# The expert choice of a fused attention and mixture-of-experts kernel, cut into two parts, with its small products at the end of their slot

## What is computed

```python
x = x + xattn(layernorm(x), ctx)      # 64 batches of 128 rows, 256 wide; 16 heads of 64; ctx is 192 wide
x = x + moe(layernorm(x))             # all 8192 rows

def moe(tokens):
    probs = softmax(tokens @ gate_w.T)                   # 8 experts
    top2_w, top2_idx = top_k(probs, 2)
    expert_out = silu(tokens @ expert_w[e].T + expert_b[e])
    mixed = sum of the two chosen expert_out, weighted by top2_w
    return mixed @ combine_w.T
```

## Time and profile before

| | us |
|---|---|
| median of three runs | 1540.31 |
| lowest, highest | 1539.81, 1540.96 |
| the profiled execution, its time | 1538.33 |
| the profiled execution, its span | 1536.6 |
| PE busy | 1489.9 (97%) |
| DVE busy | 1291.6 (84%) |
| ACT busy | 1061.8 (69%) |
| POOL busy | 939.1 (61%) |

### The profile page before, as it was taken

One profiled execution on the slowest core, in us unless ns is written; L12 is line 12 of the kernel. 1 busy time (PEld: TensorE's weight loads), 2 busy tenths in 40 slices (PEclk: granted clock), 3 DMA queues, 4 the chain that ended last, 5 costly groups with the idle time before them and its releaser, 6 DMA issues.

```text
span 1536.6 us, 38493 instructions
## 1 busy us (share of the span) xinstructions
PE 1489.9 (97%) x11680; PEld 1433.8 (93%) x11680; DVE 1291.6 (84%) x3129; ACT 1061.8 (69%) x2929; POOL 939.1 (61%) x1237
## 2 busy tenths in 40 slices
PE   6989999999999999999999999999999999999898
PEld 6989999999899999999999999989999999999887
DVE  7888888888988888888988888888888888987677
ACT  5766776766677667676677667766767667677665
POOL 4666666666655555587766455657666656655644
PEclk8999999999999999999999999999999999999999
DMA  6643443333577777544578777647887778887853
GB/s 183 201 152 94 108 110 97 94 94 97 162 226 209 220 217 223 159 114 140 172 230 244 217 231 232 203 117 220 243 250 237 230 228 248 251 243 216 285 183 110
DMA packets 181596, 287.78 MB, mean 187 GB/s; under 512 B 23697, under 2 KB 116881, under 8 KB 181137
## 3 DMA queue, kind: packets, MB, share of 16 engines
q1 hardware_dynamic: 170640, 255.94, 57.0%
q0 software_dynamic: 10752, 29.37, 6.1%
HBM read 156.51 MB, written 61.60 MB: 142 GB/s over the span
## 4 chain that ended last, share of the span: by engine, by line
PE 77%; DVE 14%; issue 3%; ACT 2%; SPq 2%; DMA 1%; POOL 0%; DVEq 0%; ACTq 0%; POOLq 0%
PE gen_ps L595 20%; PE qk_ps L595 17%; PE o_ps L595 10%; PE s_ps L595 10%; PE proj_ps L595 9%; PE pT_ps L636 6%; DVE sums L1073 2%; PE gen_ps L714 2%; PE gen_ps L681 2%; DVE neg_max L1066 2%; DVE pT_s_lo L1008 1%; DVE qk_s L1008 1%; PE gen_ps L689 1%; DMA k_s<-qk_s 1%; DVE xn L1053 1%
## 5 line engine op out<-in xcount | busy, mean ns | idle before, releaser
L851 ACT ACTIVATE stage<-s_ps,neg_max 128x128 f32<-128x128 f32 x1024 | 293.7, 376 | 32.1 <-DVE neg_max L1066 31.1
L1405 POOL CAST o_s_hi<-stage 128x256 fp32r<-128x256 f32 x256 | 102.5, 400 | 342.8 <-ACT stage L825 340.9
L1396 POOL TENSOR_TENSOR stage<-stage,inv_sums 128x512 f32<-128x512 f32 x256 | 266.1, 1039 | 36.8 <-DVE inv_sums L1075 36.4
L825 ACT CAST qk_s<-qk_ps 128x512 fp32r<-128x512 f32 x256 | 150.8, 589 | 134.3 <-PE qk_ps L595 132.7
L1066 DVE TENSOR_REDUCE neg_max<-s_ps 128x4 f32<-128x512 f32 x256 | 176.4, 689 | 66.6 <-PE s_ps L595 62.4
L595 PE MATMUL s_ps<-k_s,qk_s 128*128 128x256 f32 x1536 | 226.7, 284 | 2.8 <-DMA k_s<-qk_s 2.2
L1008 DVE TENSOR_TENSOR pT_s_lo<-pT_ps,pT_s_hi 128x512 fp32r<-128x512 f32 x256 | 173.7, 678 | 45.7 <-ACT pT_s_hi L825 41.4
L595 PEld LDWEIGHTS s_ps<-k_s,qk_s 128*128 128x128 f32 x1536 | 201.8, 189 | 3.5 <-DMA k_s<-qk_s 2.8
L1407 POOL TENSOR_TENSOR o_s_lo<-stage,o_s_hi 128x256 fp32r<-128x256 f32 x256 | 189.4, 740 | 20.8
L825 ACT CAST v_s_hi<-gen_ps 128x512 fp32r<-128x512 f32 x129 | 75.8, 588 | 179.4 <-PE gen_ps L595 179.4
L825 ACT CAST pT_s_hi<-pT_ps 128x512 fp32r<-128x512 f32 x256 | 150.4, 588 | 64.4 <-PE pT_ps L636 60.3
(11 more groups left out here) (385 smaller groups left out, 4695.2 us busy)
## 6 DMA issues: line engine op xcount, KB each, us to landing
w_block<-expert_table SPq DMA_DIRECT2D x147, 512.0 KB
k_s<-qk_s SPq DMA_DIRECT2D x512, 128.0 KB
stage<-sorted_x SPq DMA_DIRECT2D x147, 128.0 KB
sorted_y<-stage SPq DMA_DIRECT2D x147, 128.0 KB, 4.0
x_raw<-in_x SPq DMA_DIRECT2D x32, 256.0 KB
c_raw<-in_ctxT SPq DMA_DIRECT2D x32, 256.0 KB, 3.9
stage<-in_x SPq DMA_DIRECT2D x32, 256.0 KB, 3.7
x_kept<-x SPq DMA_DIRECT2D x32, 256.0 KB
```

Of the source, the lines that this page charges most:

```text
L825: last = act.copy(to, of)
L851: last = act.activation(probs[p % 2][:, k, :], s_ps[:, k * P:(k + 1) * P], ACT.Exp, bias=neg_max[p % 2][:, k:k + 1])
L1396: pool.tensor_tensor(probs[b][:, :, :], probs[b][:, :, :], inv_sums[b][:, :].unsqueeze(2).broadcast_to([P, 4, P]), ALU.mult).then_inc(prob ...
L1405: pool.tensor_copy(hi[:, :, :], o_full).then_inc(o_hi, 1)
```

## The change

The choice is cut in two, and three things move.

- On VectorE `route_top` ends with the copy to floats, which now raises a semaphore of its own (`top_copied`) instead of making VectorE wait. What stood behind it, `picks` and the two instructions for `hot`, is now `route_hot`, and stands in slot 7 between `row_max` and `qk`.
- On TensorE the `rank` products are the last general job of slot 7, behind `attend`, `project`, and the late jobs. The order of general jobs sets the banks, so the banks of the jobs in slot 7 and what each job waits for change too.
- On VectorE `route_rows` and `rows_end` stand in slot 0 of the next pair, behind the mid jobs. GpSimd writes nothing out in slot 0 and two of the four parts in slot 1.

```diff
--- before.py
+++ after.py
@@ -109,10 +109,10 @@
         self.jobs_at, order = {}, []
         for s in range(-SLOTS, self.last + 1):
             i, u = s // SLOTS, s % SLOTS
-            early, mid, late = [], [], []
+            early, mid, late, last = [], [], [], []
             for kind, k, off in ATTENTION_JOBS.get(u, []):
                 if 0 <= i + off < (SPARSE if kind == "rank" else pairs):
-                    mid.append((kind, (i + off) * per(kind) + k))
+                    (last if kind == "rank" else mid).append((kind, (i + off) * per(kind) + k))
             if s in self.turn:
                 early.append(("turn_block", self.turn[s][2]))
             if s - 1 in self.mix:
@@ -121,6 +121,7 @@
                 late.append(("expert", self.turn[s - 1][2]))
             if s - 2 in self.mix:
                 late.append(("combine", self.mix[s - 2]))
+            late += last
             self.jobs_at[s, "early"], self.jobs_at[s, "mid"], self.jobs_at[s, "late"] = early, mid, late
             order += early + mid + late
         self.place = {job: n for n, job in enumerate(order)}
@@ -313,8 +314,8 @@
         proj_ps = stack.enter_context(nc.psum_tensor("proj_ps", [P, 512], F32))
         gen_ps = [stack.enter_context(nc.psum_tensor(f"gen_ps{b}", [P, 512], F32)) for b in range(BANKS)]
 
-        x_in, c_in, xres_in, gate_in, bias_in, biased = (
-            sem(n) for n in ("x_in", "c_in", "xres_in", "gate_in", "bias_in", "biased"))
+        x_in, c_in, xres_in, gate_in, bias_in, biased, top_copied = (
+            sem(n) for n in ("x_in", "c_in", "xres_in", "gate_in", "bias_in", "biased", "top_copied"))
         w_in = [sem(f"w_in{n}") for n in range(18)]
         table_stored = [sem(f"table_stored{r}") for r in range(RING)]
         last_in = [sem(f"last_in{r}") for r in range(RING)]
@@ -1129,9 +1130,12 @@
                 for t in range(2):
                     last = dve.max_index(top_at[:, t, :], top8[:, t, :], logits[:, t, :])
                 link(last)
-                link(dve.tensor_copy(top_atf[:, :, :], top_at[:, :, 0:2]))
+                dve.tensor_copy(top_atf[:, :, :], top_at[:, :, 0:2]).then_inc(top_copied, 1)
+
+            def route_hot(j):
                 if j == 0:
                     dve.wait_ge(w_lo_pool, PROJ_BY_POOL)
+                dve.wait_ge(top_copied, j + 1)
                 picks = chosen_of(j)
                 link(dve.tensor_tensor(picks, expert_no[:, 0:E].unsqueeze(1).broadcast_to([P, 4, E]),
                                        top_atf[:, :, :].rearrange("p t k -> p (t k)").unsqueeze(2).broadcast_to([P, 4, E]),
@@ -1265,10 +1269,6 @@
                         split_lo(hi_of[kind], n + 1, [(lo, bank[:, 0:N2], hi)], drained[kind])
                     elif kind == "gate":
                         gate_logits(n, bank)
-                    elif kind == "rank":
-                        route_rows(n, bank)
-                        if n + 1 in plan.ends:
-                            rows_end(plan.ends.index(n + 1), n)
 
             for e in range(REGIONS):
                 dve.memset(expert_no[:, e:e + 1], float(e))
@@ -1307,6 +1307,8 @@
                     row_max(i, u + 1)
                 if u == 7 and nxt:
                     row_max(i + 1, 0)
+                if u == 7 and before:
+                    route_hot(i - 1)
                 if u < 5 and now:
                     qk(i, u + AHEAD)
                 if u >= 5 and nxt:
@@ -1316,6 +1318,10 @@
                     for n in range(FOR_FIRST):
                         weight_lo(n)
                 general(s, "mid")
+                if u == 0 and 0 <= i - 2 < SPARSE:
+                    route_rows(i - 2, gen_ps[plan.bank("rank", i - 2)])
+                    if i - 1 in plan.ends:
+                        rows_end(plan.ends.index(i - 1), i - 2)
                 if s in (-SLOTS, 0):
                     x_stats(i + 1)
                 if u == 5 and i >= 0 and exists(i + 2):
@@ -1475,8 +1481,9 @@
                     split_attended(i, u - 2)
                 if now:
                     normalise_probs(i, u)
-                if u < 4 and exists(i - 2) and i - 2 < SPARSE:
-                    scatter(i - 2, u)
+                if 1 <= u < 4 and exists(i - 2) and i - 2 < SPARSE:
+                    for k in (0, 1) if u == 1 else (u,):
+                        scatter(i - 2, k)
                 if s in (-SLOTS + 1, 1):
                     rsqrt(i + 1, 0)
                 if u == 6 and i >= 0 and exists(i + 2):
```

## The result

| | before | after |
|---|---|---|
| median of six runs, us | 1540.63 | 1550.43 |
| lowest, highest, us | 1539.46, 1546.29 | 1548.27, 1558.01 |
| ratio (95% interval) | | 1.0070 (1.0051 to 1.0090) |
| the profiled execution: time, span, us | 1538.33, 1536.6 | 1550.21, 1548.5 |
| PE busy, us | 1489.9 | 1495.1 |

The forecast was 1538.3 us with a range of 1532 to 1544. It was wrong: the time lies above the range, and the kernel became slower.

A forecast was written before the change was run, and what follows sets the result against it. TensorE, busy 97% of the span, was taken as the bound, so only its waits could change. Gains of 9.2 us less costs of 7.2 us gave 2.0 us less: median 1538.3 us, 8-in-10 range 1532 to 1544 us.

The forecast's parts named there:

- The step that failed: SP's waits for `clear_ready` at five chunk ends move to slot 0; costed at nothing, uncovered about a microsecond each.
- the three signs: Forecast wrong if gen_ps waits are missing, qk_ps waits over 0.3 us in slot 0, or cT_hi's wait grows over 0.2 us.
- The gain of slot 7: `attend` no longer waits for pT_s_lo held by routing work; 0.54 us a slot, 4.3 us in pairs 1 to 7 and 14.
- The rival in which `route_hot` makes a new wait: Slot 7: `route_hot` ahead of qk_s delays it, so slot 7 gives only 0.2 us; 1543.9 us, slower; chance 0.16.
- the forecast gain of 0.4 us: Slot 7 of pairs 15 and 16: late exponentials make TensorE wait in the next slot, so only 0.2 us each kept.
- The chunk ends: `count_blocks` runs earlier, shortening TensorE's wait in slot 1; with slot 7 of pairs 8 and 22, 3.7 us gained.
- The bank waits: Slot 0 of seven pairs: `turn_mixed` waits for `expert_out`, `expert` for the rank's readout; costs 4.1, 0.6 and 1.5 us.
- The second write: Slot 1: GpSimd's second write delays VectorE's normalisation of x_raw; 0.08 us at the wait for cT_hi, 12 times, 1.0 us.
- Its rival: The second write's whole hold of about 0.6 us reaches `queries_keys` in twelve pairs: 7.2 us, 1544.5 us; chance 0.1.
- The first step of that rival: Slot 1: VectorE's normalisation of x_raw would wait for GpSimd's whole write, since whoever issues first blocks the other fully.
- The sum: Whole kernel: gains of 9.2 us less costs of 7.2 us, so 2.0 us less.

The follow-up runs named there:

- first experiment: Changed kernel with the eight clearing writes at chunk ends issued in slots 1, 2 and 3 instead of 0 to 3; ratio 0.9982 to the kernel before.
- the late signal alone: Kernel before with only `rows_end`, which raises `clear_ready`, moved from slot 7 to slot 0 of the next pair, behind the mid jobs; ratio 1.0075.
- the double write alone: Kernel before with only GpSimd's writes changed: none in slot 0, two of the four parts in slot 1; ratio 0.9940.
- the last experiment: Kernel before with the double write for all pairs, and split choice with late readout only for ranks 0-6, 8-13, 18-20 and 26; 1525.65 us, ratio 0.9910.
- the readout first: Changed kernel with clearing writes in slots 1 to 3 and `row_now`, `filled` ahead of `expert_out` in slot 0; single run 1539.14 us beside 1539.59 before.
- the wait alone: Changed kernel with clearing writes in slots 1 to 3, SP still waiting for `clear_ready` in slot 0 with no write behind; ratio 1.0070 to kernel before.

## Why the prediction was wrong, step by step

**The step that failed** is the one on SP: "The waits that SP has for `clear_ready` at the five chunk ends move from slot 7 to slot 0; behind them stand the spreads of keys, which are needed a slot later. I cost them at nothing; uncovered it would be about a microsecond each." The mechanism was named, and priced by one delay with a slot of cover. (It is not the wait that moves, as this step has it, but the signal: SP waits in slot 0 in both kernels.) Measured, it is 0 at pairs 9, 17 and 23, 3.9 us at pair 27 and 8.9 us at pair 29 (first experiment against the changed kernel), 12.7 us in all. Two things were left out. The list behind the wait was not added up. From one spread of keys to the next, SP takes 6.5, 7.5, 7.1 and 5.1 us in slots 1 to 4 of pair 27 before, with next to no wait of its own in slots 1 to 3, and these slots are 8.3, 7.6, 6.7 and 5.3 us long. So a lateness of some 6 us is not made good in the next slot, nor in the ones that follow.

And the cover was not measured from issue to use. In pair 27 the keys had 9.6, 10.7, 9.9 and 8.1 us from issue to use, before, and those used in slot 5 of pair 29 had 7.0 us; where `scores` waited for them in the changed kernel, the copies had taken 4.4 to 5.8 us. That leaves 1 to 5 us of cover, less than the lateness. The length of SP's list and the time from issue to use could have been read from the profile of before. Nor was this among the rivals, so the range had no room for it, and none of the three signs by which the forecast called itself wrong came up (the start of the kernel aside): all three looked at other terms.

**The gain of slot 7** was right: 0.54 us forecast, 0.50 us measured in pairs 2 to 8 and 14 (4.73 to 4.23 us), of which slot 0 gives back 0.05 us. The instructions come as forecast. DVE in slot 7 of pair 3 after, which answers to the earlier trace rows:

```profile
182.55 0.17 DVE L1133 CAST top_atf<-top_at 128x4 f32<-128x4 uint32 x1
182.63 0.69 DVE L1074 TENSOR_REDUCE sums<-stage 128x4 f32<-128x512 f32 x1
...
183.47 0.69 DVE L1009 TENSOR_TENSOR pT_s_lo<-pT_ps,pT_s_hi 128x512 fp32r<-128x512 f32 x1
...
185.04 0.18 DVE L1140 TENSOR_TENSOR stage<-expert_no,top_atf 128x32 f32<-128x32 f32 x1
185.25 0.17 DVE L1147 TENSOR_TENSOR hot<-stage 128x16 fp32r<-128x16 f32 x1
...
185.55 0.68 DVE L1009 TENSOR_TENSOR qk_s<-qk_ps,qk_s 128x512 fp32r<-128x512 f32 x1
```

And PE there, which answers to the earlier trace rows; `attend` has no idle time before it, and the rank none either:

```profile
184.23 0.37 PE L596 MATMUL o_ps<-pT_s_hi,v_s_hi 128*128 128x256 f32 x1
...
185.77 0.25 PE L707 MATMUL gen_ps<-hot,before_s 128*128 128x16 f32 x1
```

The rival in which `route_hot` makes a new wait is refuted: `hot` takes 0.17 us, not 0.33. Pair 1, where all was late, gave 2.5 us with the slot 0 behind it, and not 0.54. In pairs 15 and 16 the forecast gain of 0.4 us was a loss of about 0.5: the rank waits for `hot` there (two waits, 0.9 us together, in the waits above), and slot 0 behind it is 0.2 us longer. The last part may not be the change's: with the late signal alone and with the double write alone, where the choice stands as before, these two slots are longer by 0.2 us too. (The reading that 1.68 us was the longest wait of `attend` is a little off: in pair 23 it was 1.74 us. Nothing hangs on it.)

**The chunk ends** gave 0.59, 0.51 and 0.60 us in slot 1 of pairs 9, 17 and 23, and 0.5 us in slot 7 of pairs 8 and 22; 2.7 us, where 3.7 were forecast. (The 0.7 us that the forecast has for pair 17 is less than its own working gives, 0.8 + 0.2 us.) The net of two parts had been right in kind: the release alone is worth 1.2 to 1.5 us (the double write alone), and with the rest of the change 0.7 to 0.9 us of it are gone again, as 0.87 us were forecast for the readout that was put ahead of `count_blocks`. Here the last experiment found a part of its gain.

**The bank waits** came where they were forecast, in exactly seven pairs, and in pair 19 they delay the two starts by 0.92 and 0.47 us, as forecast (0.92 and 0.46). As idle time the profile shows less, 0.75 and 0.31 us. PE in slot 0 of pair 19 after, which answers to the earlier trace rows:

```profile
828.67 1.09 PE L682 MATMUL gen_ps<-ident,stage 128*128 128x128 f32 x8 [0.75 <-DVE stage L1090]
...
831.50 0.50 PE L596 MATMUL gen_ps<-w_block,xbT_hi 128*128 128x256 f32 x2 [0.31 <-DVE filled L1207]
```

From the start of the scores to `turn_mixed` it is 1.64 us where it was 0.72, and `expert` is 0.47 us later behind the last product of the projections. But the slot is 1.62 us longer, not 1.38: after each wait the first products start in wider steps (the two of `expert` behind the wait take 0.34 us to the next start, 0.24 before). In pairs 18 and 24 slot 0 is longer by the full 1.6 us and not by 0.75; the 0.7 us that slot 7 of pairs 17 and 23 gained, and that I had left out, are given back there, so the net, 0.95 us each, is near the forecast. Together the seven come to 7.3 us net (19, 25 and 26 1.5 each, 18 and 24 0.95, 27 and 29 0.4 once SP is cured), where 6.2 were forecast. (For 27 and 29 the forecast takes 0.8 from 1.38 us and writes 0.3; it is 0.6. By that its costs are 7.8 us and its sum is 1.4 us.)

**The second write** cost about 0.3 us at the wait for cT_hi, and was put at 1.0. Its rival is refuted. In pair 4 after, GpSimd's second write and the two normalisations of x_raw run side by side:

```profile
195.01 0.96 POOL L1434 DMA_INDIRECT sorted_x<-xn,row_of  x1 [0.30 <-issue]
...
195.04 0.73 DVE L1054 TENSOR_SCALAR x_raw<-x_raw,mv,rstd 128x256 f32<-128x256 f32 x2
```

Two in 0.73 us is their undisturbed pace: the median of one is 0.41 us in both kernels. The first step of that rival leaned on the Trainium skill ("SBUF — State Buffer", section "Who interferes with whom"), by which, where VectorE runs in a mode that takes both ports, whoever issues first blocks the other fully. No run here shows in which mode x_raw's normalisation runs. For this instruction beside this write the trace doesn't agree: neither was held. The forecast took the two xn of the earlier trace rows (1.26 us) as a sign that this kind of instruction is held by a write. A write does run beside them, but GpSimd does something else close by:

```profile
208.45 0.75 POOL L1383 TENSOR_TENSOR cT_lo<-c_raw,cT_hi 128x256 fp32r<-128x256 f32 x1
```

Of the 64 xn of the kernel before, the 13 that run beside a write alone take 0.41 us each, as undisturbed ones do. The 9 that meet a write with this cT_lo close behind it take 0.94 us, and the 12 that meet cT_lo alone 0.79 us. So a write alone held none of them either. The ones that were held had GpSimd's work on two tensors beside them or next; why those of the second kind are held before its row begins is not shown.

**The sum.** Without the SP step the kernel of the first experiment stands 2.8 us below the kernel before (0.9982, interval 0.9963 to 1.0001); the forecast was 2.0 us below. In the traces its pairs 1 to 30 are 1.5 us shorter. That it comes out so near is in part luck. The gains measured are 2.5 us in pair 1, 3.1 in pairs 2 to 7 and 14, 0.8 in 9 and 27, -0.5 in 15 and 16, and 2.7 at the chunk ends: 8.6 us against 9.2. The costs are 7.3 to 7.6 us against 7.2, with the bank waits dearer by 1.1 and the second write cheaper by some 0.7 to 1 us. Without the 2 us that pair 1 gave beyond its forecast, for a reason that was not foreseen, nothing would be left of the gain. So the outcome was wrong by one term set to zero, and the other terms were off by up to 2 us each, with errors of both signs.

## What to carry to other kernels

When a change moves a signal later, add up what stands behind its waiter in the same in-order queue, and compare that with the length of the stage: a queue that is nearly full carries a single late wait on for several stages, and a neighbouring stage with a light list says nothing about it. Measure cover as issue to use in the busiest stage, not in stages. And where a change is made of parts, price each alone: here the double write alone gave the larger part of what the best kernel gained by the ratios (0.6 of 0.9%), and a single small instruction, moved alone, cost as much as the whole change.

## What the runs showed of the hardware

- A wait of TensorE can cost about as much again in clock. After 3.3 us of standing still the granted clock was 0.59 in the next 3 us and 0.50 in the 4 us behind them, and slot 5 of pair 29 was 6.4 us longer. With the late signal alone it was 0.57 over 4 us after a wait of 2.5 us; with the readout first, 0.66 over 5 us after one of 1.3 us; with the wait alone, 0.60 over 3 us after one of 3.1 us. The three waits of 0.9 to 1.3 us in pair 27 of the changed kernel were followed by a clock of 1.00, and one of 1.9 us with the wait alone too. What tells these apart stays open.
- With SP held in slot 0 of pair 29 (a wait of 6.2 us) the DMA share there was 0.27, where it was 0.53 before. Four to five slots later it was 0.94 to 1.01, and 0.90 before.
- A copy of keys from SBUF to SBUF, in two issues, took 4.4 to 5.8 us from its issue until the product that waited for it started (pairs 27 and 29 of the changed kernel), with a DMA share of 0.81 to 0.97 in the slots of these waits.
- In pair 19 slot 0 was longer by 0.23 us more than the two bank waits delayed their products (1.62 against 0.92 + 0.47 us).
- VectorE's normalisations of x_raw and xn beside GpSimd's indirect writes alone take 0.40 to 0.41 us, as without them; beside GpSimd's cT_lo an xn takes 0.79 us. In the earlier trace rows two small instructions of VectorE, top_w with two inputs in SBUF and the first of `count_blocks` with one, stood until GpSimd's bias had ended. Both had started 0.3 to 0.5 us before the bias did, while the write of slot 0 was still running, and what held them in that time is not shown.
